# Logits five chunks ahead, routing cut into more batches, LayerNorm bias on GpSimd, dispatches on four semaphores

## The chip, the cores and the metric

The kernel runs on one core of one Trainium2 chip. The metric is the device time of one execution in microseconds (us); lower is better.

## The reference, cut to what matters

`x` is 32 sequences of 256 rows of 128 numbers, 8192 rows in all. With `xn` the LayerNorm of `x`:

```python
hidden, gate = split(xn @ W_hg, 2)            # 256 + 256 columns
# a scan over each sequence, written in logs: h_t = a_t * h_(t-1) + v_t
a, z = sigmoid(-gate), sigmoid(gate);  v = (relu(hidden) + 0.5) * z
s = h @ W_out
shared = (silu(xn @ Sg) * (xn @ Su)) @ Sd
probs = softmax(xn @ Wr);  topk_p, topk_i = top_k(probs, 2)      # 16 experts
routed = sum over the 2 experts e of a row:  p_e * ((silu(xn @ Wg[e]) * (xn @ Wu[e])) @ Wd[e])
out = x + s * silu(routed + shared)
```

## The kernel before

The rows go through the core in two stages.

**First stage: 16 chunks of 512 rows** (a chunk is 4 tiles of 128 rows). For chunk `i` TensorE computes six products `up(i, 0..5)` with the front weights (line 908; two for each of two scan halves `j`, two for the shared expert), then `rec_down` (L919) and `shared_down` (L928) of chunk `i - 1`. ScalarE computes tanh, relu and the two affine steps (`rec_in`), the Silu (`shared_silu`), copies of the results into the row buffer `xrow` (`copy_down`). VectorE computes LayerNorm statistics (`ln_stats`), the scans (`rec_scan`, L534 and L540) and the shared product (`shared_gated`, L548). Before its `up` products a chunk must be read in: `normalise` on ScalarE, `transpose_x` on TensorE, `copy_xT` on ScalarE, `logits` on TensorE (L889), `copy_logits` on VectorE (L527). The table `READ` says which chunks are read in during which chunk: three chunks ahead of use.

The products `up` go round four PSUM banks. So `up(i, 3)` waits for `shared_gated(i - 1)` on VectorE, and `rec_down(i - 1)` waits for the scans of chunk `i - 1`.

**Routing**, on VectorE between the chunks' own work: for a batch of tiles (`BATCHES`) `route_top` and `route_second` find the two best experts; then, for each of two groups (group 0 is chunks 0 to 9, 40 tiles; group 1 is chunks 10 to 15, 24 tiles), `shift_logits`, `route_keys`, `count_keys`, the prefix sums on TensorE (`prefix`), `key_bases`, `positions`, `tile_keys`, `probabilities`. A pair of experts belongs to one of 20 "lines" of four experts each, and `positions` says in which slot of its line a row goes.

**Dispatch**, on GpSimd: for each of the 64 tiles one indirect DMA (L322) writes the tile's 128 rows of 392 numbers to their places in `slots`, in HBM. A tile needs its positions and its chunk's `copy_down`. After each eight tiles of a group GpSimd waits until all have landed (`DRAIN`), and group 1 begins only when group 0 has landed.

**Second stage: 42 pairs of slot tiles.** SP loads a pair (`load_slots`); ScalarE normalises it, TensorE transposes it (L957), multiplies with its line's weights (`gate_up`, L981, then `hidden_transpose` L993 and `slot_down` L1006), VectorE and ScalarE do the gates and sums, and GpSimd stores the rows by an indirect DMA (`store_out`, L328). Pairs 0 to 9 hold group 0 alone: their loads wait until all 40 tiles of group 0 have landed. The load of pair 10 waits for all of group 1. Twelve pairs are held at a time, so the load of pair 12 waits for the stores of pair 0; and the stores stand in GpSimd's queue behind all dispatches. The pairs' buffers lie over `xrow` of tiles 12 to 39.

Everything is written out by hand: each engine has its own queue in program order, and semaphores join them. GpSimd also makes the reciprocal standard deviations (`rstd_of`, L286 and L288), and at the start the blank rows (L316) with which `slots` is filled. The third part of the line weights (2304 KB) is loaded once the first 12 tiles are dispatched.

Of the kernel before, what the change touches and what calls it, by code (L numbers as in the profile page):

```python
# [21 lines left out]
XB = 4  # L22
RX = 12
DRAIN = 8
# [50 lines left out]
def recurrent_moe_block(nc, x, W_front, W_tail, W_lines, out, S, E, F):  # L75
# [11 lines left out]
    BATCHES = [(0, 16), (16, 32), (32, 40), (40, 56), (56, 64)]  # L87
# [6 lines left out]
    with ExitStack() as ctx:  # L94
# [18 lines left out]
        minus_half = sb("minus_half", [P, TT])  # L113

# [20 lines left out]
        var_eps = sb("var_eps", [P, TT])  # L135
        rec = sb("rec", [P, 5 * NH * CT])
# [24 lines left out]
        eq = sb("eq", [P, TB, E])  # L161
        lg2 = sb("lg2", [P, TB, E])
# [20 lines left out]
        ptmp = sb("ptmp", [P, LINES, 24])  # L183
        pos = sb("pos", [P, NT], U32)
# [26 lines left out]
        s_disp = [sem("first_rows_dispatched"), sem("group_dispatched"), sem("rest_dispatched")]  # L211
# [10 lines left out]
        CONSTS = 16  # L222
# [14 lines left out]
        def _(sp):  # L237
# [3 lines left out]
            def load_slots(n):  # L241
                if n == 0:
                    sp.wait_ge(s_disp[0], 16 * FIRST_TILES)
                    sp.wait_ge(s_disp[1], 16 * (len(TILES[0]) - FIRST_TILES))
                if n == PAIRS0:
                    sp.wait_ge(s_disp[2], 16 * len(TILES[1]))
# [7 lines left out]
            sp.wait_ge(s_blank, 2)  # L254
# [7 lines left out]
            sp.wait_ge(s_disp[0], 16 * FIRST_TILES)  # L262
# [7 lines left out]
        def _(pool):  # L270
            nc.gpsimd.memset(minus_half[:, :], -0.5).then_inc(s_const, 1)
            nc.gpsimd.memset(eps[:, :], 1e-5).then_inc(s_const, 1)
            nc.gpsimd.memset(ident[:, :], 0.0).then_inc(s_const0, 1)
# [7 lines left out]
            def rstd_of(c):  # L281
                k = c % 4
                pool.wait_ge(s_mv, c + 1)
                if c >= 1:
                    pool.wait_ge(s_rstd, c)
                nc.gpsimd.tensor_tensor(var_eps[:, :], meanvar[:, k, :, 1], eps[:, :], ALU.add).then_inc(s_ve, 1)  # L286
                pool.wait_ge(s_ve, c + 1)
# [3 lines left out]
            pool.wait_ge(s_const, 2)  # L291
# [23 lines left out]
            blank = arena[:, 0:SLOTS // 4 * ROW].rearrange("p (n w) -> p n w", w=ROW)  # L315
            nc.gpsimd.memset(blank[:, :, 0:TOKEN], 0.0).then_inc(s_blank, 1)  # L316
# [29 lines left out]
            for t in TILES[0]:  # L346
# [6 lines left out]
                if t > 0 and t % DRAIN == 0:  # L353
                    pool.wait_ge(s_disp[0], 16 * min(t, FIRST_TILES))
                    if t > FIRST_TILES:
                        pool.wait_ge(s_disp[1], 16 * (t - FIRST_TILES))
                dispatch(s_disp[0] if t < FIRST_TILES else s_disp[1], t)
            pool.wait_ge(s_disp[1], 16 * (len(TILES[0]) - FIRST_TILES))
# [3 lines left out]
            for k, t in enumerate(TILES[1]):  # L362
                if t % TT == 0:
                    pool.wait_ge(s_she, t // TT + 1)
                if k > 0 and k % DRAIN == 0:
                    pool.wait_ge(s_disp[2], 16 * k)
                dispatch(s_disp[2], t)
# [4 lines left out]
        def _(act):  # L372
            act.dma_start(w_front[:, :], W_front).then_inc(s_wfront, 16)
            act.dma_start(w_tail[:, :], W_tail).then_inc(s_wtail, 16)

# [92 lines left out]
            for i in range(NCH):  # L468
# [9 lines left out]
                if i == 7:  # L478
                    exponentials(0)
                if i == 13:  # L480
# [20 lines left out]
        def _(dve):  # L501
# [15 lines left out]
            def ln_bias(c):  # L517
                k = c % 4
                dve.wait_ge(s_rstd, c + 1)
                dve.wait_ge(s_mv, c + 1)  # L520
# [570 lines left out]
```

## Time and profile before

| | before |
|---|---|
| median of 3 runs | 379.81 us (379.62 to 379.94) |
| the profiled execution, its time / its span | 379.33 us / 377.6 us |
| busy TensorE (PE) / VectorE (DVE) / ScalarE (ACT) / GpSimd (POOL) | 305.8 / 248.8 / 243.1 / 194.8 us |
| moved by DMA | 63.82 MB, mean 169 GB/s |

The profile comes from one execution. The span runs from the first instruction to the last, and the execution's own time is 1.7 us more. PEld is TensorE's weight load. In a timeline row stand the start, the length, the engine, the line, the operation, output and input, and in brackets how long the engine was idle before it and what released it. A busy TensorE is one whose matmuls are in the pipe; ends of matmuls are modelled.

### The profile page before, as it was taken

How to read it: one execution, taken by the hardware profiler on the slowest of the kernel's cores; microseconds unless marked ns; L12 is line 12 of the kernel's file. 1: busy time of each engine (PE TensorE's matmuls, PEld its weight loads, DVE VectorE, ACT ScalarE, POOL GpSimd, SP SyncE). 2: the span in 40 equal slices, each digit the busy share in tenths (PEclk: the TensorE clock that was granted, in tenths of full speed). 3: DMA queues.
4: the chain of work that ended last, by engine and by line, in shares of the span. 5: the costliest groups of instructions: out<-in, count | busy, mean ns of one | idle time of the engine just before them, and what ended most of it. 6: DMA issues, size and time to landing. Idle time of an engine off the chain costs nothing.

```text
span 377.6 us, 5994 instructions
## 1 busy us (share of the span) xinstructions
PE 305.8 (81%) x1532; PEld 199.0 (53%) x1532; DVE 248.8 (66%) x636; ACT 243.1 (64%) x518; POOL 194.8 (52%) x210
## 2 busy tenths in 40 slices
PE   0779899999989999993009993899999999999810
PEld 0446566666656666652004762566656656666510
DVE  2476778899999977979003662576776776776720
ACT  1876888888998886881015671667667667667410
POOL 3982124130003752766763757775565565665670
PEclk9998999999999999998556999699999999999965
DMA  8979996920000329223369425665545545420000
GB/s 245 262 336 391 442 440 237 428 104 1 1 2 11 138 109 336 86 106 149 128 198 405 165 109 172 219 220 162 147 147 163 162 129 158 142 67 27 16 1 0
DMA packets 27983, 63.82 MB, mean 169 GB/s; under 512 B 3701, under 2 KB 22784, under 8 KB 27056
## 3 DMA queue, kind: packets, MB, share of 16 engines
q1 hardware_dynamic: 20880, 45.78, 34.8%
q0 software_dynamic: 6784, 17.06, 12.2%
q10 hardware_dynamic: 288, 0.60, 0.5%
q8 instruction: 15, 0.25, 0.3%
q14 instruction: 16, 0.13, 0.1%
HBM read 29.52 MB, written 35.21 MB: 171 GB/s over the span
## 4 chain that ended last, share of the span: by engine, by line
PE 52%; POOL 16%; DMA 9%; issue 8%; ACT 6%; DVE 5%; POOLq 0%; SPq 0%; ACTq 0%
PE p_u L981 18%; PE p_u L908 10%; POOL slots L322 10%; PE p_s L1006 10%; DMA slots<-arena,pos 6%; PE p_sh L993 4%; PE p_s L919 4%; PE p_xt L957 2%; DMA arena<-slots 2%; PE p_sh L928 2%; POOL arena L316 2%; PE p_lg L889 2%; POOL out L328 2%; DVE rec L779 1%; ACT arena L436 1%
## 5 line engine op out<-in xcount | busy, mean ns | idle before, releaser
L328 POOL DMA_INDIRECT out<-arena x84 | 89.3, 1063 | 47.8 <-DVE arena L803 31.4
L908 PE MATMUL p_u<-xT,w_front 128*128 128x512 f32 x192 | 94.2, 616 | 0.8 <-ACT xT L392 0.7
L322 POOL DMA_INDIRECT slots<-arena,pos x64 | 66.9, 1045 | 41.6 <-DMA slots<-arena,pos 23.8
L981 PE MATMUL p_u<-arena 128*128 x168 | 83.4, 620 | 0.0
L779 DVE TENSOR_TENSOR rec<-p_u,rec 128x512 f32<-128x512 f32 x42 | 29.0, 692 | 71.7 <-ACT rec L450 67.0
L1006 PEld LDWEIGHTS p_s<-arena,rec 128*128 128x128 f32 x336 | 41.7, 193 | 34.5 <-issue 34.5
L436 ACT ACTIVATE arena<-arena 128x128 f32<-128x128 f32 x84 | 36.4, 481 | 30.5 <-DMA arena<-slots 30.5
L1006 PE MATMUL p_s<-arena,rec 128*128 x336 | 48.2, 287 | 3.0 <-DVE arena L794 1.4
L908 PEld LDWEIGHTS p_u<-xT,w_front 128*128 128x128 f32 x192 | 34.0, 196 | 27.5 <-issue 26.1
L957 PE MATMUL p_xt<-ident,arena 128*128 128x128 f32 x84 | 17.2, 288 | 32.2 <-ACT arena L436 29.9
L981 PEld LDWEIGHTS p_u<-arena 128*128 128x128 f32 x168 | 30.1, 200 | 21.7 <-issue 21.7
L540 DVE TENSOR_TENSOR_SCAN rec<-rec 128x512 f32<-128x512 f32 x32 | 39.2, 1224 | 1.1
L461 ACT ACTIVATE arena<-arena 128x256 f32<-128x256 f32 x42 | 17.4, 417 | 31.0 <-DVE arena L794 31.0
L919 PEld LDWEIGHTS p_s<-w_tail,rec 128*128 128x128 f32 x256 | 30.9, 192 | 7.9 <-issue 6.7
L456 ACT ACTIVATE rec<-p_sh 128x512 f32<-128x512 f32 x42 | 25.1, 596 | 13.4 <-PE p_sh L993 13.3
L787 DVE TENSOR_TENSOR rec<-rec,arena 128x256 f32<-128x256 f32 x84 | 32.0, 422 | 1.4
L919 PE MATMUL p_s<-w_tail,rec 128*128 128x128 f32 x256 | 31.2, 275 | 0.4 <-ACT arena L419 0.4
L286 POOL TENSOR_TENSOR var_eps<-meanvar,eps 128x4 f32<-128x4 f32 x16 | 5.2, 324 | 47.1 <-DVE meanvar L514 46.3
L957 PEld LDWEIGHTS p_xt<-ident,arena 128*128 128x128 f32 x84 | 10.8, 148 | 34.1 <-ACT arena L436 33.0
L534 DVE SCALAR_TENSOR_TENSOR rec<-rec 128x512 f32<-128x512 f32 x32 | 21.8, 682 | 8.9 <-ACT rec L408 8.9
L450 ACT ACTIVATE rec<-p_u 128x512 f32<-128x512 f32 x42 | 24.3, 578 | 4.8 <-PE p_u L981 4.8
L384 ACT ACTIVATE xn<-arena 128x128 f32<-128x128 f32 x64 | 26.1, 492 | 0.0
(124 smaller groups left out, 450.6 us busy)
## 6 DMA issues: line engine op xcount, KB each, us to landing
slots<-arena SPq DMA_DIRECT2D x4, 4116.0 KB, 27.1
arena<-slots SPq DMA_DIRECT2D x42, 392.0 KB, 3.3
arena<-in_W_lines SPq DMA_DIRECT2D x2, 2688.0 KB, 11.8
arena<-in_x SPq DMA_DIRECT2D x16, 256.0 KB, 5.3
arena<-in_W_lines SPq DMA_DIRECT2D x1, 2304.0 KB, 9.5
out<-arena POOLq DMA_INDIRECT x84, 2.4
slots<-arena,pos POOLq DMA_INDIRECT x64
w_front<-in_W_front ACTq DMA_DIRECT2D x1, 392.0 KB, 3.6
```

The costliest lines, as they stand in the source:

```text
L322: pool.indirect_dma_start(slots, index, xrow[:, t], None).then_inc(signal, 16)
L328: pool.indirect_dma_start(out, index, xg[:, n % RX, h, X], None, bounds_check=T - 1, oob_is_err=False)\
L384: last = nc.scalar.activation(xn[:, c % XN, t], row[:, X], ACT.Identity, bias=row[:, NBIAS:NBIAS + 1], scale=row[:, RSTD:RSTD + 1])
L436: last = nc.scalar.activation(xs[:, n % 2, h], row[:, X], ACT.Identity, bias=row[:, NBIAS:NBIAS + 1], scale=row[:, RSTD:RSTD + 1])
L540: nc.vector.tensor_tensor_scan(rec_h[:, c % 2, j], rec_a[:, j], rec_v[:, j], 0.0, ALU.mult, ALU.add)\
L779: nc.vector.tensor_tensor(hg[:, :, :], p_u[:, n % 2 * 2:n % 2 * 2 + 2, 2 * P:4 * P], sil[:, n % 2], ALU.mult)\
L787: last = nc.vector.tensor_tensor(hw[:, n % 2, h].rearrange("p (b f) -> p b f", b=BLOCK), hg[:, h].rearrange("p (b f) -> p b f", b=BLOCK), ...
L908: nc.tensor.matmul(p_u[:, n % 4], w_front[:, UPS[q]:UPS[q] + P], xT[:, c % XB], start=True, stop=True)\
L919: last = nc.tensor.matmul(p_s[:, t * P:(t + 1) * P], rec_h[:, c % 2, j, t * P:(t + 1) * P], w_tail[:, j * P:(j + 1) * P], start=j == 0, st ...
L957: last = nc.tensor.transpose(p_xt[:, h * P:(h + 1) * P], xs[:, n % 2, h], ident[:, :])
L981: last = nc.tensor.matmul(p_u[:, n % 2 * 2 + h], xsT[:, n % 2, h * P:(h + 1) * P], w_lines[:, bass.DynSlice(line_at[2 * n + h], 4 * P)], s ...
L1006: last = nc.tensor.matmul(p_s[:, h * P:(h + 1) * P], hT[:, n % 2, 2 * h + b], w_lines[:, bass.DynSlice(at + (4 + b) * P, P)], start=b == 0 ...
```

## The change

- `READ` reads two chunks in during each of the chunks 0 to 3, and from then on is five chunks ahead. There are six `xT` buffers instead of four. The logits of two chunks read in together go to one PSUM bank and are copied by one `copy_logits`. `STATS` moves the LayerNorm statistics along.
- Routing of group 0 is in five batches (12, 8, 8, 8, 4 tiles), one during each of the chunks 1 to 5, and its later steps stand two chunks earlier each. Group 1's are two chunks earlier as well: its positions, which stood behind the work of chunk 15, now stand inside chunk 13.
- The LayerNorm bias is made on GpSimd from two small products, not on VectorE (`ln_bias`).
- About half of the blank rows are made by VectorE at its very start.
- ScalarE runs a small Silu first, ahead of all work.
- Dispatches use four semaphores in turn, and from the fifth on each waits until the fourth before it has landed. `DRAIN` and the wait between the groups go.

```diff
-XB = 4
+XB = 6
-DRAIN = 8
+WINDOW = 4
-    BATCHES = [(0, 16), (16, 32), (32, 40), (40, 56), (56, 64)]
+    BATCHES = [(0, 12), (12, 20), (20, 28), (28, 36), (36, 40), (40, 56), (56, 64)]
-        READ = {0: [1, 2], 1: [3], 2: [4, 5]} | {i: [i + 3] for i in range(3, NCH - 3)}
-        STATS = {-1: [3], 0: [4, 5], 1: [6, 7], 2: [8], 3: [9, 10], 4: [11, 12], 5: [13], 6: [14, 15]}
+        READ = {i: [2 * i + 1, 2 * i + 2] for i in range(4)} | {i: [i + 5] for i in range(4, NCH - 5)}
+        STATS = {i: [2 * i + 5, 2 * i + 6] for i in range(-1, 5)} | {5: [15]}
...
                 nc.gpsimd.tensor_tensor(var_eps[:, :], meanvar[:, k, :, 1], eps[:, :], ALU.add).then_inc(s_ve, 1)
+                nc.gpsimd.tensor_tensor(minus_mean[:, :], meanvar[:, k, :, 0], minus_one[:, :], ALU.mult).then_inc(s_ve, 1)
...
+                nc.gpsimd.tensor_tensor(rows[:, :, NBIAS], minus_mean[:, :], rows[:, :, RSTD], ALU.mult).then_inc(s_nb, 1)
...
-            nc.gpsimd.memset(blank[:, :, 0:TOKEN], 0.0).then_inc(s_blank, 1)
+            nc.gpsimd.memset(blank[:, BLANK_BY_DVE:, 0:TOKEN], 0.0).then_inc(s_blank, 1)
...
-            def dispatch(signal, t):
+            def dispatch(t):
+                if t >= WINDOW:
+                    pool.wait_ge(s_disp[t % WINDOW], 16 * (t // WINDOW))
                 index = bass.IndirectOffsetOnAxis(pos[:, t:t + 1], 0)
-                pool.indirect_dma_start(slots, index, xrow[:, t], None).then_inc(signal, 16)
+                pool.indirect_dma_start(slots, index, xrow[:, t], None).then_inc(s_disp[t % WINDOW], 16)
...
+            act.wait_ge(s_const, 1)
+            nc.scalar.activation(silu_s[:, 0:TT], minus_half[:, :], ACT.Silu)
...
-                if i == 7:
+                if i == 5:
                     exponentials(0)
-                if i == 13:
+                if i == 11:
                     exponentials(1)
...
+            nc.vector.memset(blank[:, 0:BLANK_BY_DVE, 0:TOKEN], 0.0).then_inc(s_blank, 1)
...
+                if 1 <= i <= 5:
+                    route_top(i - 1)
+                    route_second(i - 1)
...
+                if i == 13:
+                    key_bases(1)
+                    positions(1, 0)
...
-                if i == 15:
-                    key_bases(1)
-                    positions(1, 0)
+                if i == 12:
                     probabilities(1)
-                    tile_keys(1)
```

What this does to the queues, at the places that matter. On GpSimd, the dispatches from the first tile on, before the change (names in brackets are the semaphores waited for: `first_rows_dispatched` is the drain):

```order
L322 DMA slots<-arena,pos 10752x392 [waits positions_ready,shared_copied,slots_blanked,block_weights_ready]
L322 DMA slots<-arena,pos 10752x392 x3
L322 DMA slots<-arena,pos 10752x392 [waits shared_copied]
L322 DMA slots<-arena,pos 10752x392 x3
L322 DMA slots<-arena,pos 10752x392 [waits first_rows_dispatched,shared_copied]
L322 DMA slots<-arena,pos 10752x392 x3
```

and in the changed kernel:

```order
L335 DMA slots<-arena,pos 10752x392 [waits positions_ready,shared_copied,slots_blanked,block_weights_ready]
L335 DMA slots<-arena,pos 10752x392 x3
L335 DMA slots<-arena,pos 10752x392 [waits rows_dispatched0,shared_copied]
L335 DMA slots<-arena,pos 10752x392 [waits rows_dispatched1]
L335 DMA slots<-arena,pos 10752x392 [waits rows_dispatched2]
L335 DMA slots<-arena,pos 10752x392 [waits rows_dispatched3]
```

One wait in eight dispatches has become a wait at each dispatch, for the fourth before it.

On VectorE, the end of the first stage before the change: the shared product of chunk 14, the scans and the product of chunk 15, and only then group 1's `key_bases` (`cnt`, first row) and its `positions`:

```order
L548 TENSOR_TENSOR prod<-p_u,silu_s 128x512
L534 SCALAR_TENSOR_TENSOR rec<-rec 128x512
L540 SCALAR_TENSOR_TENSOR rec<-rec 128x512
L534 SCALAR_TENSOR_TENSOR rec<-rec 128x512
L540 SCALAR_TENSOR_TENSOR rec<-rec 128x512
L548 TENSOR_TENSOR prod<-p_u,silu_s 128x512
L706 SCALAR_TENSOR_TENSOR cnt<-p_lg,rem 128x20
```

and in the changed kernel the end of group 1's `positions` in chunk 13, followed by the scans and the product of chunk 13, `tile_keys`, and chunk 14:

```order
L760 TENSOR_TENSOR moved<-p_lg,room 128x480
L761 TENSOR_TENSOR ptmp<-p_lg,base 128x480
L763 SCALAR_TENSOR_TENSOR moved<-moved,delta 128x480
L767 TENSOR_TENSOR ptmp<-ptmp,moved 128x480
L769 TENSOR_TENSOR ptmp<-ptmp,oh 128x480
L772 TENSOR_REDUCE pos<-ptmp 128x24
L535 SCALAR_TENSOR_TENSOR rec<-rec 128x512
L541 SCALAR_TENSOR_TENSOR rec<-rec 128x512
L535 SCALAR_TENSOR_TENSOR rec<-rec 128x512
L541 SCALAR_TENSOR_TENSOR rec<-rec 128x512
L549 TENSOR_TENSOR prod<-p_u,silu_s 128x512
L730 TENSOR_SCALAR le<-ends,tile_row 128x60
```

Group 1's positions have moved from behind the last chunk's work to ahead of three chunks' scans and products.

## Rows read from the trace of the kernel before

**Rows 1.** The page's 40 slices: TensorE's granted clock, in tenths.

```profile
PEclk9998999999999999998556999699999999999965
```

**Rows 2.** Timeline of TensorE in the second stage.

```profile
195.61 0.69 PE L957 MATMUL p_xt<-ident,arena 128*128 128x128 f32 x2 [22.78 <-ACT arena L436]
...
198.99 3.62 PE L981 MATMUL p_u<-arena 128*128 x4
...
226.57 1.88 PE L981 MATMUL p_u<-arena 128*128 x4
...
237.69 3.62 PE L981 MATMUL p_u<-arena 128*128 x4
...
243.11 1.88 PE L981 MATMUL p_u<-arena 128*128 x4
```

**Rows 3.** The chain that ended last, in time: start, length, what.

```profile
189.06 2.58 DMA slots<-arena,pos
...
230.40 2.58 DMA slots<-arena,pos
```

**Rows 4.** Waits up to 200 us: total, times, longest.

```profile
POOL slots L322 <- DMA slots<-arena,pos: 15.8, 4, 7.5
```

**Rows 5.** Timeline of GpSimd.

```profile
13.83 6.90 POOL L316 MEMSET arena<- 128x8148 f32 x1
...
120.63 1.28 POOL L322 DMA_INDIRECT slots<-arena,pos  x1 [0.39 <-POOL arena L339]
...
158.53 1.83 POOL L322 DMA_INDIRECT slots<-arena,pos  x1 [0.30 <-issue]
...
208.52 0.96 POOL L322 DMA_INDIRECT slots<-arena,pos  x1 [5.62 <-DMA slots<-arena,pos]
```

**Rows 6.** The page's costliest groups: busy, mean ns of one, idle before.

```profile
L322 POOL DMA_INDIRECT slots<-arena,pos x64 | 66.9, 1045 | 41.6 <-DMA slots<-arena,pos 23.8
```

**Rows 7.** Timeline of TensorE in the first stage.

```profile
25.54 1.04 PE L889 MATMUL p_lg<-w_front,xT 128*128 128x16 f32 x8 [2.71 <-DVE lg L527]
...
59.48 1.96 PE L908 MATMUL p_u<-xT,w_front 128*128 128x512 f32 x4
```

**Rows 8.** Timeline of ScalarE in the first stage.

```profile
8.22 1.28 ACT L384 ACT_TABLE_LOAD   x1 [8.22 <-DVE arena L522]
...
37.25 3.18 ACT L384 ACTIVATE xn<-arena 128x128 f32<-128x128 f32 x8
...
48.85 1.64 ACT L384 ACTIVATE xn<-arena 128x128 f32<-128x128 f32 x4
```

**Rows 9.** Timeline of VectorE in the first stage.

```profile
60.41 0.86 DVE L508 BATCH_NORM_STATS2 stats<-arena 128x6 f32<-128x128 f32 x4
...
63.29 0.69 DVE L534 SCALAR_TENSOR_TENSOR rec<-rec 128x512 f32<-128x512 f32 x1 [0.44 <-ACT rec L408]
...
87.89 0.28 DVE L560 TENSOR_REDUCE m<-lg 128x8 f32<-128x128 f32 x1
...
91.12 0.20 DVE L634 TENSOR_TENSOR p<-m 128x40 f32<-128x40 f32 x1
...
97.06 0.19 DVE L597 TENSOR_SCALAR i<-r 128x80 uint32<-128x80 f32 x1
...
102.82 0.67 DVE L534 SCALAR_TENSOR_TENSOR rec<-rec 128x512 f32<-128x512 f32 x1
...
106.61 0.20 DVE L527 COPY lg<-p_lg 128x64 f32<-128x64 f32 x1
106.73 0.68 DVE L548 TENSOR_TENSOR prod<-p_u,silu_s 128x512 f32<-128x512 f32 x1
...
111.84 1.08 DVE L771 TENSOR_REDUCE pos<-ptmp 128x20 uint32<-128x400 f32 x1
...
170.20 0.17 DVE L706 SCALAR_TENSOR_TENSOR cnt<-p_lg,rem 128x20 uint32<-128x20 f32 x1
...
175.19 1.27 DVE L771 TENSOR_REDUCE pos<-ptmp 128x24 uint32<-128x480 f32 x1
```

More of the change, by code:

```diff
@@ L210, in recurrent_moe_block @@
         s_pread, s_p01, s_spot = sem("prefix_read"), sem("probabilities_ready"), sem("spots_marked")
-        s_disp = [sem("first_rows_dispatched"), sem("group_dispatched"), sem("rest_dispatched")]
+        s_disp = [sem(f"rows_dispatched{k}") for k in range(WINDOW)]
         s_xg = [sem(f"slot_rows_landed{k}") for k in range(RX)]
@@ L242, in load_slots @@
                 if n == 0:
-                    sp.wait_ge(s_disp[0], 16 * FIRST_TILES)
-                    sp.wait_ge(s_disp[1], 16 * (len(TILES[0]) - FIRST_TILES))
+                    for k in range(WINDOW):
+                        sp.wait_ge(s_disp[k], 16 * (len(TILES[0]) // WINDOW))
                 if n == PAIRS0:
-                    sp.wait_ge(s_disp[2], 16 * len(TILES[1]))
+                    for k in range(WINDOW):
+                        sp.wait_ge(s_disp[k], 16 * (NT // WINDOW))
                 if n >= RX:
@@ L253, in _ @@
                 load_x(c)
-            sp.wait_ge(s_blank, 2)
+            sp.wait_ge(s_blank, 3)
             for q in range(4):
@@ L261, in _ @@
                 sp.dma_start(w_lines[:, k * half:(k + 1) * half], W_lines[:, k * half:(k + 1) * half]).then_inc(s_lines, 16)
-            sp.wait_ge(s_disp[0], 16 * FIRST_TILES)
+            for k in range(WINDOW):
+                sp.wait_ge(s_disp[k], 16 * (FIRST_TILES // WINDOW))
             sp.dma_start(w_lines[:, OWN_LINES * LINE:], W_lines[:, OWN_LINES * LINE:]).then_inc(s_lines, 16)
@@ L272, in _ @@
             nc.gpsimd.memset(eps[:, :], 1e-5).then_inc(s_const, 1)
+            nc.gpsimd.memset(minus_one[:, :], -1.0).then_inc(s_const, 1)
             nc.gpsimd.memset(ident[:, :], 0.0).then_inc(s_const0, 1)
@@ L352, in _ @@
                     pool.wait_ge(s_she, t // TT + 1)
[L353 to L358, printed above, removed]
+                dispatch(t)
             block_weights(1)
@@ L361, in _ @@
             pool.wait_ge(s_pos, 3)
-            for k, t in enumerate(TILES[1]):
+            for t in TILES[1]:
                 if t % TT == 0:
                     pool.wait_ge(s_she, t // TT + 1)
-                if k > 0 and k % DRAIN == 0:
-                    pool.wait_ge(s_disp[2], 16 * k)
-                dispatch(s_disp[2], t)
+                dispatch(t)
             for n in range(PAIRS):
@@ L880, in transpose_x, with logits @@
                 last.then_inc(s_xt, 1)
-            def logits(c):
-                pe.wait_ge(s_xTe, c + 1)
-                if c >= 1:
-                    pe.wait_ge(s_lgc, c)
-                if c in (12, 13):
-                    pe.wait_ge(s_pos, c - 11)
-                for t in range(TT):
-                    last = nc.tensor.matmul(p_lg[:, t * E:(t + 1) * E], xT[:, c % XB, t * P:(t + 1) * P], w_front[:, 0:E],
-                                            start=True, stop=True)
-                last.then_inc(s_lg, 1)
+            def logits(chunks):
+                first = chunks[0]
+                pe.wait_ge(s_xTe, chunks[-1] + 1)
+                if first >= 1:
+                    pe.wait_ge(s_lgc, first)
+                if first in (12, 13):
+                    pe.wait_ge(s_pos, first - 11)
+                for c in chunks:
+                    for t in range(TT):
+                        at = ((c - first) * TT + t) * E
+                        last = nc.tensor.matmul(p_lg[:, at:at + E], xT[:, c % XB, t * P:(t + 1) * P], w_front[:, 0:E],
+                                                start=True, stop=True)
+                last.then_inc(s_lg, len(chunks))
             def up(c, q):
@@ L1015, in _ @@
                 if i == 0:
-                    logits(0)
+                    logits([0])
                 for c in read(i)[:1]:
@@ L1027, in _ @@
                 up(i, 5)
-                for c in read(i):
-                    logits(c)
-                if i == 8:
+                if read(i):
+                    logits(read(i))
+                if i == 6:
                     prefix(0, 0)
-                if i == 9:
+                if i == 7:
                     prefix(0, 1)
-                if i == 14:
+                if i == 12:
                     prefix(1, 0)
```

85 lines of the change are left out of this document (36 added, 49 removed).

## The prediction

> **What bounds the kernel now.** I read the page's slices first: the granted clock stands near full except in two dips after the middle, where TensorE had nothing to do [rows 1]. TensorE's timeline shows both holes. It stops at 172.83 (195.61 less the 22.78 idle before it), when the first stage is done, and its first `gate_up` is at 198.99. Then nine pairs go by, `gate_up` of pair 8 at 226.57, and that of pair 9 only at 237.69 [rows 2]: 11.1 us for one step, where the eight steps before took 27.58, 3.45 each. Both restarts find the clock at half (1.2 GHz): the four matmuls take 3.62 instead of 1.88 [rows 2].
>
> The chain that ended last says what was late: the last dispatch of group 0, at 189.06, and the last of group 1, at 230.40, each landing 2.58 later [rows 3]. So the holes hang on GpSimd's row of dispatches, which begins at 120.63 [rows 5]. The 64 dispatches are busy 66.9, 1.045 each [rows 6], and 0.30 lies between two [rows 5], so one takes 1.345. On top come drains: 15.8 in four waits by 200 us [rows 4], and 5.62 in one more [rows 5]. The other waits are of engines that have slack. Hence the kernel is bound by TensorE up to 172.8, by GpSimd to 199 and again to 237.7, and by TensorE's pairs to the end.
>
> **The change, in order of time.** Small things at the start. The table load on ScalarE at 8.22 lies ahead of the first normalise and costs 1.28 [rows 8]; the early Silu takes it from the path, and GpSimd's two more small products give back some 0.2, by guess between nothing and 0.3, so chunk 0 starts 1.0 earlier. The Trainium skill (ScalarE: Activation LUTs, What ACT_TABLE_LOAD costs) puts a drain of about 1.38 us beside each load, some 2.66 in all; by it the start would gain 1.4 more. The trace has 1.28, and I count that. VectorE's memset stands before any x has landed and hides; without that cover it costs what GpSimd saves, half of 6.90 [rows 5]. The 2.71 for which the logits of chunk 2 waited for a copy [rows 7] goes, since two chunks are copied as one. So chunk 1, whose first `up` followed those logits at 26.4 (25.54 and some 0.9), starts near 22.7.
>
> Chunks 1 to 3 now read in two each. The one such chunk in full flow before, chunk 2, took ScalarE 11.6 from one normalise to the next, 37.25 to 48.85 [rows 8]. Three of these: chunk 4 starts at 57.5, before at 59.48 [rows 7]; I take 58, 1.5 earlier.
>
> From there VectorE leads. Its work for a chunk: two chunks' statistics 2.4 (60.41 to 63.29, less 0.44 idle); routing of eight tiles 3.2 (87.89 to 91.12); both scans 3.8 (102.82 to 106.61); copy and product 0.8 (106.61 to 107.41) [rows 9]. Chunk 4: 10.2. Chunk 5, with four tiles (2.6, taken between eight tiles' 3.2 and half of it), the shift (about 1) and one chunk's statistics: 9.4. TensorE's own pace is 9.16, from VectorE's marks 60.41 and 87.89, three chunks apart [rows 9]. The VectorE lag of 1 to 2 us is absorbed: `up(i, 3)` waits for the product of the chunk before, and it stands 3 us into the chunk. So VectorE is done with chunk 5 at 58.9 + 10.2 + 9.4 = 78.5. In chunk 6 come keys and counts, 5.8 (97.06 to 102.82), and scans 3.8: 88.1, and for the copy TensorE's prefix waits. Probabilities (1.8) and product, 90.5; bases and positions of group 0, 5.5 (107.41 to 112.92) [rows 9]: **positions at 96**, where the first dispatch was at 120.63. The dispatches start 24.6 earlier. Scans and copy follow, chunk 8 starts at about 100.
>
> Chunks 8 to 10 at 9.16, then 11 and 12 at some 8 (no logits, no transposes): TensorE enters chunk 13 at 144. There stands the price: probabilities 1.2 and group 1's bases and positions, 6.3 (170.20 to 176.46) [rows 9], were behind the last chunk and cost nothing; now they stand ahead of chunk 13's scans. VectorE's product of chunk 12 ends near 146.8, that of chunk 13 at 146.8 + 1.2 + 6.3 + 3.8 + 0.6 = 158.7, and `up(14, 3)` waits for it from 154.7: **a hole of 4 us**. The clock fell to half after the idle of 2.71 in chunk 0 too (the 8 in the slices) [rows 1, 7], so I add 1 for it. Behind it TensorE has 16 us of matmuls left. First stage ends: 175.6, 2.8 later than before.
>
> GpSimd: 96 + 40 x 1.345 = 149.8, and the load of the third part of the line weights, which made the longest drain, still stops it: 7.5 less 0.3 [rows 4]. 157.0. No drain otherwise: a dispatch lands 2.58 after its start [rows 3], and four steps are 5.4, so the new wait is over when reached. Block weights 1.3, then 24 x 1.345 = 32.3, and 5.3 (5.62 less 0.30) for the loads of ten pairs that run beside it, as they did at 208.52 [rows 5]: the last dispatch leaves near 195, landed at 198. `shared_copied` of chunk 15 is there at 176.5, its tiles are not due before 184. Group 0 has landed at 159, its pairs are loaded long before 175.6.
>
> So the second stage starts when the first ends. From TensorE's last matmul: shared copy and normalise about 1.5, then at most the 3.4 from first transposes to first `gate_up` [rows 2], of which half was waiting for a load; 3.2 in all (up to 4.9). `gate_up(0)` at 178.8, pair 8 at 206.4, pair 9 at 209.9. Pair 10's slots are landed at 198 and loaded by 202, in time. In the old run pair 10 came 5.4 after pair 9 [rows 2], now 3.5: at 213.4 instead of 243.11, **29.7 earlier**. All behind it keeps its pace: the stores start at 196 and need 2.6 for a pair, below 3.5.
>
> Sum, against the profiled execution's own time: 379.33 - 29.7 = 349.6. The median of the runs lies 0.48 above that execution: **350**.
>
> **Rivals.**
>
> *VectorE becomes the bound.* For it: without the lag's absorption each chunk pays VectorE's excess whole, plus the 0.44 idle: chunks 4, 5, 6, 7, 11, 12 and 13 by 1.5, 0.7, 3.4, 2.1, 0.9, 3.6 and 3.1, together 15; the forecast holds some 9 of it. With clock loss in a second place, 9 more: 359. Against it: three microseconds of slack in each chunk. Chance 0.09.
>
> *Pair 10 waits still.* The dispatches now lie beside the busiest VectorE. One took 1.83 at 158.53 [rows 5]. Pair 10's slots must land by some 203, 5 later than I have them. If the mean step rises from 1.345 to 1.55, the last dispatch leaves 13 later, at 208, and `gate_up(9)`, 7.3 behind it as before (237.69 less 230.40), is at 215.5: 5.6 later, and a cold clock 1.9: 357. Against it: the mean of 1.045 already holds 24 dispatches beside a VectorE at work. The Trainium skill (SBUF — State Buffer, SBUF: two separate sides) says that some VectorE operations lock GpSimd out of a shared port, so that it cannot write descriptors until they end. By that rule this rival comes true; the trace has stretched dispatches, but none here is held for longer than 1.83. Chance 0.07.
>
> *The window is the new drain; slower.* Each dispatch waits for the fourth before it. If landing takes as long as in the longest drain, 7.5 and some 0.7 to restart, four dispatches take 8.2, 2.05 each: 96 + 64 x 2.05 + 1.3 = 228.5, and beside the ten pairs' loads 5.3 more: 234, against 230.40. `gate_up(9)` comes 3.5 later than before: 383. It decides from a landing of 7 us (last dispatch at 230). Against it: 2.58 in both rows [rows 3]. Chance 0.03.
>
> *No gain:* positions that come early while something else holds the dispatches (blank rows, `shared_copied`). At 96 seven chunks are copied, 28 tiles or 37 us of dispatches, so nothing does: 379.8, chance 0.01.
>
> **How the numbers follow.** Forecast 0.80 with its own range of 345 to 355: 2 for each clock dip that may not come, 2 for the start, 1.7 for the transition, 3 for the hole in chunk 13, either way. To hold 8 in 10 with the first two rivals at its upper side: 345 to 358. A change of 0.2% (0.8 us) is about what a measurement of this kernel can tell from none. Faster 0.96, within it 0.01, slower 0.03.
>
> **What would show it.** First dispatch near 96, last near 195, gaps of 0.30 between them but for one of about 7 during the weight load; `gate_up(0)` within 5 us of the first stage's last matmul; no idle of TensorE at pair 9; a wait of `up` for VectorE's `prod` of about 4 us in chunk 14. The prediction is wrong if dispatches step by 1.5 or more, if the chunks 1 to 7 end later than 100, or if pairs run slower than 3.5.

## The result, and the profile after

The changed kernel took **354.18 us** (median of 4 runs, 349.93 to 354.81), the kernel before 379.72 beside it (4 runs, 379.57 to 379.94): a ratio of 0.9303, 95% interval 0.923 to 0.9376. Forecast were 350, with 345 to 358. The profiled execution took 354.0 us with a span of 352.2, where the forecast for it was 349.6. Runs more than 1.5% above the fastest of the same kernel are left out of every ratio but not of the medians, and two kernels of the experiments, `again` and `p1_later`, had five such runs of six and have no ratio.

The page's slices of the changed kernel, against [rows 1], then its share by engine of the chain that ended last, and its group row of the row writes (the dispatches), against [rows 6]:

```profile
PEclk9999999999989999998998999999999999999985
...
PE 66%; DVE 13%; issue 9%; ACT 6%; POOL 2%; DMA 1%; POOLq 0%; DVEq 0%; ACTq 0%
...
L335 POOL DMA_INDIRECT slots<-arena,pos x64 | 70.9, 1107 | 30.1 <-issue 16.2
```

The two deep dips of the clock are gone, and so are the holes of which they were the trace. GpSimd has 2% of the chain, and the idle time ahead of its row writes is mostly issue.

Timeline of GpSimd, the row writes: the first, the one behind the weight load, the first and the last of group 1 (start, length, tiles, idle before and what ended it):

```profile
98.91 1.87 POOL L335 DMA_INDIRECT slots<-arena,pos  x1 [5.69 <-DVE pos L772]
...
127.26 1.46 POOL L335 DMA_INDIRECT slots<-arena,pos  x1 [3.85 <-DMA slots<-arena,pos]
...
162.38 1.00 POOL L335 DMA_INDIRECT slots<-arena,pos  x1 [0.28 <-POOL arena L352]
...
195.03 0.96 POOL L335 DMA_INDIRECT slots<-arena,pos  x1 [0.30 <-issue]
```

The first leaves 21.7 us earlier than in [rows 5], the last 35.4 earlier than in [rows 3]. Timeline of TensorE, first stage and entry into the second, against [rows 7] and [rows 2]:

```profile
17.98 2.97 PE L903 MATMUL p_u<-xT,w_front 128*128 128x512 f32 x4
...
90.13 0.35 PE L938 MATMUL p_lg<-oh,tri 128*128 128x400 bf16 x1 [2.21 <-DVE lg L528]
...
101.84 0.35 PE L938 MATMUL p_lg<-oh,tri 128*128 128x400 bf16 x1 [2.00 <-issue]
...
102.32 3.45 PE L903 MATMUL p_u<-xT,w_front 128*128 128x512 f32 x4
...
147.51 2.82 PE L903 MATMUL p_u<-xT,w_front 128*128 128x512 f32 x6
...
162.65 1.19 PE L903 MATMUL p_u<-xT,w_front 128*128 128x512 f32 x2 [3.98 <-DVE prod L549]
...
179.87 1.06 PE L923 MATMUL p_sh<-w_tail,prod 128*128 128x128 f32 x8
182.38 0.44 PE L952 MATMUL p_xt<-ident,arena 128*128 128x128 f32 x2 [1.45 <-ACT arena L444]
...
184.72 3.22 PE L976 MATMUL p_u<-arena 128*128 x4
...
214.91 1.88 PE L976 MATMUL p_u<-arena 128*128 x4
...
218.47 1.88 PE L976 MATMUL p_u<-arena 128*128 x4
```

The last two rows are `gate_up` of pairs 9 and 10: 3.56 apart, with no idle. (Ahead of `gate_up(n)` stand the transposes of pair n + 1, so it is `gate_up(9)` that a late pair 10 holds up.) Pair 10 starts 24.6 us earlier than in [rows 2], and the span is 25.4 shorter. The first stage, which ended at 172.8 before, ends near 180.9 (179.87 and 1.06). Timeline of VectorE where that time is lost, the products of chunks 12 and 13 with the last of the positions of group 1 between them:

```profile
149.79 0.67 DVE L549 TENSOR_TENSOR prod<-p_u,silu_s 128x512 f32<-128x512 f32 x1
...
151.65 0.17 DVE L707 SCALAR_TENSOR_TENSOR cnt<-p_lg,rem 128x20 uint32<-128x20 f32 x1
...
156.38 1.27 DVE L772 TENSOR_REDUCE pos<-ptmp 128x24 uint32<-128x480 f32 x1
...
161.85 0.66 DVE L549 TENSOR_TENSOR prod<-p_u,silu_s 128x512 f32<-128x512 f32 x1
```

12.1 us from product to product with no idle of VectorE, and TensorE, whose chunk takes 9.2 or less, waits 3.98 at 162.65.

### The profile page after: what moved, and what is told of

It reads as the page before. It is cut to its first block, busy times and chain, and to the rows that moved or that the text cites. A ratio compares the mean times of both kernels' runs of the same rounds, so it can differ in the third digit from the quotient of the medians.

```text
span 352.2 us, 6022 instructions
## 1 busy us (share of the span) xinstructions
PE 307.0 (87%) x1532; PEld 199.6 (57%) x1532; DVE 253.7 (72%) x637; ACT 242.7 (69%) x518; POOL 210.1 (60%) x243
## 4 chain that ended last, share of the span: by engine, by line
PE 66%; DVE 13%; issue 9%; ACT 6%; POOL 2%; DMA 1%; POOLq 0%; DVEq 0%; ACTq 0%
PE p_u L976 20%; PE p_u L903 13%; PE p_s L1001 13%; PE p_s L914 6%; PE p_sh L988 5%; PE p_xt L952 3%; PE p_sh L923 3%; DVE rec L535 2%; ACT xn L392 2%; PE p_lg L884 2%; PE p_xt L871 2%; POOL out L341 2%; DVE prod L549 1%; DMA arena<-in_x 1%; DVE stats L516 1%
## 5 line engine op out<-in xcount | busy, mean ns | idle before, releaser
L341 POOL DMA_INDIRECT out<-arena x84 | 90.5, 1077 | 58.3 <-DVE arena L804 43.0
L335 POOL DMA_INDIRECT slots<-arena,pos x64 | 70.9, 1107 | 30.1 <-issue 16.2
L976 PE MATMUL p_u<-arena 128*128 x168 | 80.4, 602 | 0.0
L903 PEld LDWEIGHTS p_u<-xT,w_front 128*128 128x128 f32 x192 | 34.9, 199 | 34.7 <-issue 32.8
L976 PEld LDWEIGHTS p_u<-arena 128*128 128x128 f32 x168 | 29.2, 194 | 20.6 <-issue 20.6
L469 ACT ACTIVATE arena<-arena 128x256 f32<-128x256 f32 x42 | 17.4, 416 | 32.4 <-DVE arena L795 32.4
L914 PEld LDWEIGHTS p_s<-w_tail,rec 128*128 128x128 f32 x256 | 32.4, 200 | 7.0 <-issue 5.8
L464 ACT ACTIVATE rec<-p_sh 128x512 f32<-128x512 f32 x42 | 25.1, 597 | 12.2 <-PE p_sh L988 12.1
L914 PE MATMUL p_s<-w_tail,rec 128*128 128x128 f32 x256 | 32.8, 284 | 0.4 <-ACT arena L427 0.4
L535 DVE SCALAR_TENSOR_TENSOR rec<-rec 128x512 f32<-128x512 f32 x32 | 21.7, 677 | 9.3 <-ACT rec L416 9.1
L294 POOL TENSOR_TENSOR var_eps<-meanvar,eps 128x4 f32<-128x4 f32 x16 | 8.3, 521 | 30.6 <-DVE meanvar L522 29.4
L458 ACT ACTIVATE rec<-p_u 128x512 f32<-128x512 f32 x42 | 24.2, 577 | 2.8 <-PE p_u L976 2.8
L988 PE MATMUL p_sh<-ident,rec 128*128 128x128 f32 x168 | 25.3, 273 | 0.3 <-DVE rec L788 0.3
L407 ACT ACTIVATE rec<-p_u 128x512 f32<-128x512 f32 x32 | 18.8, 589 | 6.1 <-PE p_u L903 4.4
```

What stands on the lines that cost most here:

```text
L341: pool.indirect_dma_start(out, index, xg[:, n % RX, h, X], None, bounds_check=T - 1, oob_is_err=False)\
L903: nc.tensor.matmul(p_u[:, n % 4], w_front[:, UPS[q]:UPS[q] + P], xT[:, c % XB], start=True, stop=True)\
L914: last = nc.tensor.matmul(p_s[:, t * P:(t + 1) * P], rec_h[:, c % 2, j, t * P:(t + 1) * P], w_tail[:, j * P:(j + 1) * P], start=j == 0, st ...
L976: last = nc.tensor.matmul(p_u[:, n % 2 * 2 + h], xsT[:, n % 2, h * P:(h + 1) * P], w_lines[:, bass.DynSlice(line_at[2 * n + h], 4 * P)], s ...
L988: last = nc.tensor.transpose(p_sh[:, (2 * h + b) * P:(2 * h + b + 1) * P], hw[:, n % 2, h, b * P:(b + 1) * P], ident[:, :])
```

## The experiments

Three comparisons of four kernels, each kernel with 6 runs beside 11 of the kernel before. Conditions differed: the kernel before took 382.6 us in the second, but 389.5 and 389.6 in the first and third. In these two, the traces of all eight kernels hold stalls that no engine of the core explains; a time is compared only inside its comparison, and the second carries the argument. (Where the expectations speak of a first comparison they mean the measurement above, and their second is the first one here.)

### Second comparison (kernel before: 382.58 us, 377.49 to 383.83)

**again2**, no edit.

> The changed kernel once more, unaltered, as the common measure for the three kernels beside it. In the first comparison it took 354.2 us, in the second, beside an old kernel that itself took 389.5 instead of 379.7, it took 380.7 with stalls of 4 to 12 us on ScalarE, VectorE and TensorE that no engine of the core explains. Theory A (the stalls came from that chip's surroundings and fall on whichever kernel runs): here 350 to 356 if the old kernel takes near 380. Theory B (four row writes of GpSimd always in flight, with no drain between them, delay something that the other engines fetch, and the first profile was lucky): 365 to 385 whatever the old kernel takes.

352.21 us (350.03 to 354.64), ratio 0.9235 (0.9174 to 0.9295). Theory A held here. (Its times spread over 4.6 us, as the first measurement's over 4.9; what sets them apart was not traced.) Its trace repeats the changed kernel's: wait for the product 3.99 at 162.62, last row write at 195.51.

**p1_later2**:

```
-                if i == 13:
+                if i == 14:
                     key_bases(1)
                     positions(1, 0)
-                if i == 14:
+                if i == 15:
                     tile_keys(1)
```

> The changed kernel with the positions of group 1 taken by VectorE one chunk later (chunk 14 instead of 13) and their tile keys in chunk 15. In the trace of the changed kernel TensorE waits 3.98 us at 162.65 for the product of chunk 13, which stood behind 8 us of positions on VectorE, and then runs four matmul groups at half clock (about 1.9 us). Theory A (that work is placed one chunk too early: VectorE enters chunk 13 without slack): the wait goes or falls under 1 us, the first stage ends 4 to 5 us sooner, and the time is 3.5 to 5.5 us less than the changed kernel beside it. Rival B (VectorE is the bound of those three chunks wherever the work stands): the wait reappears at the product of chunk 14 with 3 to 4 us, and the time is within 1 us. Rival C (positions come later, so the last row write comes later than pair 10 is wanted): last row write near 205, a wait ahead of pair 10, time 0 to 5 us more.

346.64 us (345.56 to 349.52), ratio 0.9123 (0.9065 to 0.9181): 5.6 us under `again2`, with no run in common. Timelines of this kernel, TensorE's wait, GpSimd's first write of group 1, and its last:

```profile
165.37 1.10 PE L903 MATMUL p_u<-xT,w_front 128*128 128x512 f32 x2 [1.44 <-DVE prod L549]
...
161.69 1.92 POOL L335 DMA_INDIRECT slots<-arena,pos  x1 [2.58 <-DVE pos L772]
...
195.37 0.96 POOL L335 DMA_INDIRECT slots<-arena,pos  x1 [0.30 <-issue]
```

Theory A held in its mechanism: the wait falls from 3.99 to 1.44 (not under 1, as I had it), and with 5.6 us the time is just above my 3.5 to 5.5. The row writes now wait 2.58 for the positions, and it costs nothing, as the last one leaves where it did and no pair waits. Not all of the gain is the edit's. The two traced executions lie 8.2 apart (353.79 and 345.56). This one had full pace earlier at the start, worth 2.2 (below), and enters chunk 13 at 144.93 where `again2` does at 147.45: 2.5 that the edit did not make. From there to the end of the first stage (174.19 against 180.91) it gains 4.2 more: 2.6 by the wait, and 1.5 because the sixteen `rec_down` matmuls behind it take 1.95 and not 3.44. That is the edit's. The rest comes at the entry into the second stage, where the first `gate_up` takes 1.96 against 3.30; whether the edit brought that is not shown.

**drain_back2**: the changed kernel with the drained dispatch in place of the window:

```
-                if t >= WINDOW:
-                    pool.wait_ge(s_disp[t % WINDOW], 16 * (t // WINDOW))
...
+                if t > 0 and t % DRAIN == 0:
+                    pool.wait_ge(s_disp[0], 16 * min(t, FIRST_TILES))
```

> The changed kernel with the old dispatch: groups of eight row writes, each group awaited, on three semaphores. Theory A (window and drain differ only by the pauses of a queue that is off the chain): within 1.5 us of the changed kernel beside it, either sign, near 353; the last row write leaves near 203 instead of 194, and pair 10 of the slots, wanted at 215, still does not wait. Theory B (the window is what brings the stalls): 5 to 12 us less than the changed kernel beside it, as in the second comparison, where it took 368.9 against 380.7.

359.32 us (357.6 to 362.85), ratio 0.9456 (0.9388 to 0.9524): 7.1 more than with the window. Theory B is refuted here (the window is the faster), and so is theory A, which had the time within 1.5 us and pair 10 without a wait. GpSimd's waits for landings (total, times, longest), the last row write, then TensorE's transposes of pair 10 and `gate_up(9)` in this kernel:

```profile
POOL slots L331 <- DMA slots<-arena,pos: 22.3, 6, 6.8
...
209.12 0.96 POOL L331 DMA_INDIRECT slots<-arena,pos  x1 [0.31 <-issue]
...
216.52 0.69 PE L955 MATMUL p_xt<-ident,arena 128*128 128x128 f32 x2 [5.44 <-ACT arena L447]
217.00 3.18 PE L979 MATMUL p_u<-arena 128*128 x4
```

The last write is 13.6 later than with the window, 209.12 against 195.51, although the first left 2.2 earlier in this execution (96.66 against 98.87). `gate_up(9)` was due at 211 and starts at 217.00, 9.4 behind `gate_up(8)` (207.57) where steps are 3.55; the first four matmuls after the idle take 3.18 instead of 1.88.

**window2**: `WINDOW = 2` for `WINDOW = 4`.

> The changed kernel with two row writes in flight instead of four. In the trace of before a row write lands 2.58 us after its issue and the next can follow 1.345 us after the one before it. Theory A (a window bites once landing takes longer than its steps): with two, a write waits until its second forerunner has landed, 2.58 + about 0.3 us per two steps of 1.345 = 2.69, so the step stays between 1.35 and 1.6 us; group 0 of 40 writes ends 0 to 10 us later, the last write leaves between 194 and 203, pair 10 does not wait, and the time is within 1 us of the changed kernel beside it. Rival (landing beside the weight load and the loads of x is 4 us and more, so that two in flight give a step of 2.5): the last write leaves after 215, pairs 9 and 10 wait, and the time is 5 to 15 us more.

364.74 us (363.5 to 367.77), ratio 0.9571 (0.9518 to 0.9624): 12.5 more than with four. The rival won. Timeline of GpSimd in group 1 of this kernel, its last write, TensorE's transposes of pair 10, and two writes of group 1 in the chain that ended last (start, and the time to landing):

```profile
180.16 0.96 POOL L335 DMA_INDIRECT slots<-arena,pos  x1 [2.37 <-DMA slots<-arena,pos]
183.13 0.96 POOL L335 DMA_INDIRECT slots<-arena,pos  x1 [2.01 <-DMA slots<-arena,pos]
186.18 0.96 POOL L335 DMA_INDIRECT slots<-arena,pos  x1 [2.09 <-DMA slots<-arena,pos]
...
220.29 0.96 POOL L335 DMA_INDIRECT slots<-arena,pos  x1 [0.31 <-DMA slots<-arena,pos]
...
227.46 0.69 PE L952 MATMUL p_xt<-ident,arena 128*128 128x128 f32 x2 [14.25 <-ACT arena L444]
...
180.16 5.28 DMA slots<-arena,pos
...
186.18 6.25 DMA slots<-arena,pos
```

My mistake was to take two landings at 2.58 as the cost. At 180 to 190, while the first ten pairs were being loaded, they landed after 5.28 and 6.25, and with two in flight each step is half of that and the restart: about 3 us. Group 0 lost still more without any such loads: it took 75.2 us from its first write to its last (172.24 less 97.08) against 59.9 (158.72 less 98.87), with one wait of 7.50 at the weight load, where four in flight left 3.37, and many others of 0.6 to 1.9. The mean step in group 1 is 1.95 ((220.29 - 175.51) / 23), with four in flight 1.44 ((195.51 - 162.35) / 23), drained 1.70 ((209.12 - 170.01) / 23). So the window must cover not the landing of [rows 3] alone but its spread.

### First comparison (kernel before: 389.54 us, 387.47 to 393.37)

**window_only**: the kernel before, with only the dispatch of the change.

> The kernel before with only the new dispatch (four semaphores, each waiting for its fourth forerunner). Theory (in the old kernel the drains are on the path, and the routing sets the start at 120.6): last dispatch of group 0 at 181 to 182 instead of 189.1, first gate_up at 192 instead of 199; last dispatch of group 1 near 221 instead of 230.4, and gate_up of pair 9 near 229 instead of 237.7: time 371, 8 to 9 us less. Rival (the new waits stop GpSimd as often as the drains did, since landings beside the loads take 5 to 8 us): 377 to 380.

379.31 us (376.29 to 381.82), ratio 0.974 (0.9688 to 0.9792): 10.2 us less. Its row writes go from 123.10 to 218.95, against 120.63 to 230.40 in the trace of before, with 7.5 us of waits for landings where 23.8 stood [rows 6]. The theory held for the queue (last write at 218.95, forecast near 221; first `gate_up` at 193.77, forecast 192) and for the gain (8 to 9 forecast). `gate_up(9)` came only after 235 and not near 229, as ScalarE stood still for 9.28 us before it. The time falls into the rival's 377 to 380 only because the kernel before was slow as well; its mechanism, waits as long as the drains, is not there.

**again**, no edit:

> The changed kernel once more, nothing altered. One of its four runs took 349.93 us and the others 354.0 to 354.8, so its times scatter by 4 us where the kernel before scatters by 0.4. Theory (the clock of TensorE falls at holes of 2 to 4 us in the first stage, and how long it stays down differs from run to run): the runs spread over 349 to 355 again, in one or two clusters. Rival (one odd run): all runs within 354 to 355.

380.69 us (369.58 to 387.9), 26.5 more than the first measurement of the same kernel. Neither the theory (349 to 355) nor the rival came. The waits of its trace, ScalarE's and VectorE's; "remote" is a wait for which the trace has no releaser:

```profile
ACT silu_s L422 <- remote: 12.6, 2, 7.8
ACT arena L427 <- remote: 6.2, 1, 6.2
...
DVE lg L528 <- remote: 13.9, 2, 12.2
DVE prod L549 <- remote: 6.2, 2, 4.3
```

No such row stands in `again2` or in the changed kernel's first trace. ScalarE's `silu_s` had its input from TensorE and stood still for 7.75 us; the row writes went on in steps of 1.27 meanwhile.

**drain_back**, as `drain_back2`.

> The changed kernel with the old dispatch: three semaphores, a drain after each eight tiles and between the groups. Theory (with routing two chunks earlier GpSimd has slack, and the window is worth nothing by itself): four more drains of 2.4 to 3.4 less 0.3 and the one between the groups, so the last dispatch leaves at 205 to 208 instead of 193.8; pair 10 is loaded at 213 at the latest and is due at 216, so the time is 354, within 1 us. Rival (dispatches are still close to the bound): pair 9 waits, the clock falls, time 357 to 362.

368.92 us (367.22 to 371.9), ratio 0.9473 (0.9426 to 0.952). The median is 11.8 under that of `again`, but the lowest of the six times of `again`, 369.58, lies within this kernel's range: which of the two is faster here is not shown. The last write leaves at 209.79, where I had 205 to 208.

**p1_later**, as `p1_later2`.

> The changed kernel with key_bases(1) and positions(1, 0) in chunk 14 instead of 13 and tile_keys(1) in chunk 15 instead of 14, so that probabilities and positions of group 1 don't stand ahead of the same chunk's scans. Theory (VectorE's excess in chunk 13 makes the hole of 3.98 us at up(14, 3) and the slow clock behind it, some 2 us more): the hole shrinks to 1.5 us or less, the first stage ends near 175.5 instead of 180.8, group 1's dispatches start 4 us later without harm, the time is 348.5 to 350. Rival (VectorE's total work is what counts, the hole only moves to chunk 15): first stage ends at 180 and the time stays at 354. Second rival (the later dispatches make pair 10 wait): idle of TensorE at pair 9, time above 354.

384.6 us (373.81 to 390.37), no verdict: its own spread, 16.6 us, is wider than the effect asked for.

### Third comparison (kernel before: 389.57 us, 386.22 to 394.0)

**p1_split** leaves `key_bases(1)` in chunk 13, with `positions(1, 0)` in 14 and `tile_keys(1)` in 15; **p1_drain** joins the edits of `p1_later2` and `drain_back2`.

> The changed kernel with the positions of group 1 cut in two: their bases (nine small operations, 1.8 us) stay in chunk 13, the six wide ones (4.9 us) go to chunk 14, the tile keys to chunk 15. With the whole of it in chunk 14 (6.6 us of work) TensorE still waited 1.44 us for the product of chunk 14, and the kernel took 346.6 us where the changed kernel took 352.2. Theory (VectorE's slack in chunk 14 is 1.44 us too small for 6.6 us, and the 0.65 us that it idles in chunk 13 are taken by the bases): the wait goes or is under 0.3 us, VectorE's product of chunk 13 comes up to 1.2 us later and TensorE waits 0 to 0.5 us for it; the time is 0.9 to 1.5 us under that of the kernel with both in chunk 14, a ratio to the kernel of before of 0.907 to 0.911. Rival (the waits only change places): the same 1.4 us in sum at the products of chunks 13 and 14, ratio 0.912 to 0.914.

> Positions of group 1 one chunk later and the old dispatch in drained groups of eight. With the drained dispatch alone pair 10 of the slots waited 5.44 us and the time was 359.3; with the later positions alone no pair waited and it was 346.6. Theory (the drained dispatch makes the last row write the bound, at 209.1, whatever TensorE does before): the last row write leaves at 209 to 211, pair 10 waits 7 to 10 us, and the time is 357 to 361, so that the later positions gain nothing here. Rival (the two gains add): 353 to 355, with a wait of 5 us or less ahead of pair 10.

380.58 us (375.77 to 388.1), ratio 0.9735 (0.967 to 0.98), and 369.5 us (368.58 to 371.09), ratio 0.9483 (0.9436 to 0.9531). `p1_split` tells nothing of its question. TensorE's only wait for a product in chunks 13 to 15 is 0.45 us, but ScalarE had lost 7.72 us before, and VectorE thereby had time. `p1_drain` is 11.1 faster than its neighbour with the window, by the ratios 9.8, with no run in common. Its last write leaves at 209.30, as in `drain_back2` (209.12), which is what the theory said of the rows. Of its time and the wait of pair 10, as of the rival's, nothing can be said: stalls of up to 6.5 us lie between the pairs. Whether the two gains add where there are no stalls is left open.

**no_silu** takes out the early Silu:

```
-            nc.scalar.activation(silu_s[:, 0:TT], minus_half[:, :], ACT.Silu)
```

> The changed kernel without the small early Silu on ScalarE, so that the table of that function is loaded at its first real use, behind the first matmuls of chunk 0. In the trace of before that load took 1.28 us at 8.22, and the first normalisation stood behind it. Theory A (the load then stands on the chain once more): the first matmul of chunk 0 starts 0.9 to 1.3 us later than at 11.95 and everything behind with it; time 1 to 1.3 us more. Rival B (the load falls into a wait of ScalarE for the first loads of x, or behind the first matmuls, where ScalarE has slack): the first matmul starts within 0.2 us of 11.95 and the time is the same.

382.81 us (381.9 to 385.85), ratio 0.9834 (0.9777 to 0.9892). The changed kernel did not run in this comparison, and only the first 100 us are free of stalls and can be read. Timeline of ScalarE, then of TensorE, in this kernel:

```profile
8.41 1.28 ACT L390 ACT_TABLE_LOAD   x1 [8.41 <-POOL arena L301]
9.71 1.65 ACT L390 ACTIVATE xn<-arena 128x128 f32<-128x128 f32 x4
...
13.27 3.41 PE L901 MATMUL p_u<-xT,w_front 128*128 128x512 f32 x4 [0.69 <-ACT xT L398]
```

The load is on the chain again, and the first `up` starts at 13.27 instead of 11.95, 1.32 later: theory A, as far as this row. But the transposes of chunk 4 stand where they stood in the changed kernel (30.66 and 30.50): TensorE's matmuls ran at full pace from 16.5 here and from about 20.5 there. So in this pair of executions the gain was lost again; `p1_later2`, with the early load and full pace from 16.3, has the same transposes at 28.27.

**bias_back** puts LayerNorm's bias back on VectorE:

```
-                nc.gpsimd.tensor_tensor(rows[:, :, NBIAS], minus_mean[:, :], rows[:, :, RSTD], ALU.mult).then_inc(s_nb, 1)
...
+                nc.vector.scalar_tensor_tensor(out=rows[:, :, NBIAS], in0=meanvar[:, k, :, 0], scalar=-1.0,
+                                               in1=rows[:, :, RSTD], op0=ALU.mult, op1=ALU.mult).then_inc(s_nb, 1)
```

> The changed kernel with LayerNorm's bias computed on VectorE as before (one operation a chunk, behind the first scan of the chunk after the statistics) instead of by two operations on GpSimd. Theory A (only the first chunks feel it, where VectorE and GpSimd hand work to and fro): VectorE waits for GpSimd between the statistics of chunks 0, 1 and 2 at the start, the first transpose stays within 0.3 us, and the chunks that follow start 0 to 1 us later; from chunk 3 on nothing changes; time 0 to 1.5 us more, not to be told from the changed kernel. Rival B (the bias on VectorE makes it late in every chunk): waits for VectorE's products in chunks 1 to 5 on TensorE, time 3 us and more above. Rival C (it was GpSimd's two operations that cost, by the port it shares with VectorE): 0.5 to 2 us less.

381.53 us (379.87 to 385.16), ratio 0.9799 (0.9736 to 0.9863). Again only the start can be read; TensorE's first `up` in this kernel:

```profile
11.63 3.78 PE L911 MATMUL p_u<-xT,w_front 128*128 128x512 f32 x4 [0.69 <-ACT xT L395]
```

0.32 *earlier* than at 11.95: on GpSimd the bias costs chunk 0 one more small operation ahead of the power that makes the reciprocal standard deviation and one behind it, where VectorE does it in 0.17. Chunks 1 to 3 are not slower for it (the transposes that each waits for follow 11.6 apart, as in the changed kernel), so by this trace nothing speaks for the move to GpSimd. Theory A had VectorE's waits for GpSimd at the start (1.52 and 1.42), but not the sign: the first transposes come 0.33 earlier, at 9.85 against 10.18.

## Why the prediction was right, and where it was off

**What was late, and that it would go.** Right. The chain of before hung on GpSimd's writes; their first comes 21.7 earlier and their last 35.4, and neither hole is left. `drain_back2` and `window2` show the dependence: there the last write comes 13.6 and 24.8 later than in `again2`, and the hole at pair 10 is back.

**The first stage: 175.6 forecast, 180.9 came.** This is the mis-sized term. It came 5.3 late, and the later terms gave 0.9 back, which makes the 4.4 us between 354.0 and 349.6. Its parts, each from rows above:

- Chunk 1 at 24.64, not 22.7. The start did move by 1.1 (11.95 against 13.07), but the matmuls of the second group took 2.97 and the pace was half until 20.5, where in before it was full from 16.65. In `p1_later2` and `drain_back2`, with the same code up to there, the same groups took 1.88, at 16.77 and 16.41, and all that follows is 2.2 us earlier (the transposes of chunk 4 at 28.27 and 28.24, against 30.50). I had no term for that in the sum, only 2 in the range. It differs between executions of one program (last section) and was no part of the change. The granted clock of the slice reads 9 of 10 in all of them, so the row of durations shows it, not the slices.
- Chunk 4 at 60.28, not 58: the same 2.3, carried on.
- Chunks 4 to 7 took 42.0, as forecast (100 less 58). The prefix matmuls of group 0 now stand on TensorE's chain, waiting 2.21 at 90.13 and 2.00 at 101.84; the sum had this time as VectorE's. Chunk 8 so starts at 102.32 and not at 100, which is past the mark that I had set as a sign of being wrong (chunks 1 to 7 ending later than 100).
- Chunk 13 at 147.51, not 144: the 2.3, and 1.5 in chunk 8, where the second wait is followed by four matmuls in 3.45 instead of 1.96. That half pace was the term missing.
- The hole at `up(14, 3)`: 4 forecast, 3.98 measured, and `p1_later2` shows that it hangs on where the positions of group 1 stand. Behind it half pace took 1.7, not 1, and from the hole's end to the end of the stage it is 18.3, where 17 were forecast.

**The row writes.** First at 98.9 instead of 96, last at 195.0, as forecast (195), by errors that cancel, which is luck: the mean step of group 0 was 1.53 ((158.74 - 98.91) / 39), of which 3.6 us are the weight load's stop (7.2 forecast), the rest steps of 1.44, not 1.345; and in group 1 the pair loads took little: 23 steps in 32.65 us, where 1.345 and 5.3 us of stops make 36. Writes of 1.3 to 1.9 us stand among those of 0.96 in the traces, and they add up to the 0.1 by which the mean step grew, not to the 0.2 that the rival of a late pair 10 needed. The Trainium skill (SBUF — State Buffer, SBUF: two separate sides) says that GpSimd cannot write descriptors while some VectorE operations hold a shared port; the longest write in the changed kernel's trace is 1.87, and that VectorE stretched it is not shown.

**The transition and the pairs.** 3.8 us from the last matmul of the first stage to `gate_up(0)` (184.72 less 180.93), forecast 3.2. Ten pairs in 33.75, forecast 34.6; from pair 6 on the steps are 3.55. Pair 10 does not wait.

**The table load.** 1.28 off the path was right by `no_silu` (1.32). The Trainium skill (ScalarE: Activation LUTs, What ACT_TABLE_LOAD costs) would have made it 2.66. The trace of `no_silu` agrees on the load, 1.28, but has no drain beside it: only a gap of 0.02 lies between the load and the first normalise.

**What each part was worth.** From the second comparison: with early routing, LayerNorm and start alone (drained dispatch) 23.3 us, which no run divides among the three; the window on top 7.1; the window alone, in the first comparison, 10.2. How far the two overlap is not shown, since the 10.2 stand under other conditions. Both move the last row write, on which `gate_up(9)` hangs until TensorE is the later. Where it hung, it started 7.9 behind the last write (217.00 less 209.12). In the changed kernel that would be 202.9, an estimate, and TensorE comes to it at 214.91: 12 us in hand. In `p1_later2` it comes at 206.46, and 3.2 are left. Next in line is VectorE in chunks 12 to 14, with 1.44 still.

**What stays open** are the stalls of the first and third comparison. What is measured: the kernel before loses 7 us in them (389.5 against 382.6), the changed kernel with the drained dispatch 9.6 (368.9 against 359.3), with the window 28.5 (380.7 against 352.2; 17.4 by the lowest time of `again`). They sit on ScalarE, VectorE and TensorE, most of them in the stretch of the row writes, at the same instruction at the same time in `again` and `p1_split` (118.18 and 118.22 us, 7.75 and 7.72 long), and at another place in kernels whose code is of another length (`bias_back` at 158.19, `no_silu` at 159.93, 10.3 and 10.4 long). That speaks for something tied to the position in the program; one guess is the fetch of instructions, delayed when row writes follow each other without a pause. Against it, the transfers that the page marks as instructions took as much with stalls as without (in `again` and in `again2` 0.3% of the 16 engines' span for 15 transfers on one queue), and drained kernels stall too (`drain_back` for 5.28 us, `p1_drain` for 6.52). The second and third comparison were made on a chip of the same number, so the chip alone does not decide it. The cause stays open. So the verdict on the window holds for the conditions of the second comparison; under those of the third a drained kernel was the faster by some 10 us (`p1_drain` against `p1_split`, which differ also in where `key_bases(1)` stands), and the first gives no verdict.

## What to carry to other kernels

When work is moved earlier to release a queue, price the place it goes to as carefully as the place it leaves: 7 us of routing behind the last chunk cost nothing, ahead of chunk 13's scans they cost 4 and the half pace behind it, and one chunk later 1.4. The version with that one step put a chunk later, 346.6 us, beats both kernels in the second comparison. A window of writes in flight should cover the spread of their landing, not the median; two in flight covered 2.58 us on paper, met landings of up to 6.25, and lost 12.5 us.

## What the runs showed of the hardware that was not expected

The time to full pace at the start of the program differs between executions of identical code. Timeline of TensorE, the second group of four `up` matmuls, in `p1_later` and in `p1_later2`, which are the same kernel:

```profile
17.96 3.43 PE L903 MATMUL p_u<-xT,w_front 128*128 128x512 f32 x4
...
16.77 1.88 PE L903 MATMUL p_u<-xT,w_front 128*128 128x512 f32 x4
```

The first group took 3.74 to 3.78 in both; from the second on, one ran at half pace and the other at full, and the transposes of chunk 4 stand at 30.94 and 28.27, 2.7 us apart. `drain_back` and `drain_back2`, also the same kernel, took 3.59 and 1.88. The granted clock of the slice is at its highest digit each time. And one kernel took 352.2 us in one comparison and 380.7 in another, in which the kernel before changed only from 382.6 to 389.5: a ratio measured in one place need not hold in another.
